# Down projection of a ViT layer: the residual add moves from VectorE into accumulating DMAs

## The reference

```
h = patches(x) @ W.T + b                        # 32 x 256 tokens x 256
h = h + attention(layernorm(h))                 # 16 heads, causal
xq = fake_quant(layernorm(h), clip_x)           # one scale for the whole tensor: max|.| over all tokens
a  = silu(xq @ q(w_gate).T) * (xq @ q(w_up).T)  # 704 hidden features
h = h + fake_quant(a, clip_down) @ q(w_down).T  # again one scale for the whole tensor
```

## Time and profile before

| | |
|---|---|
| median of 3 runs | 898.87 us (895.33 to 903.66) |
| span of the profiled execution | 901.6 us |
| pass C in that execution | about 824 to 901.6 us, 77.6 us |
| VectorE busy in pass C | 67.6 of 77.6 us |
| TensorE / ScalarE busy in pass C | 48.6 / 43.7 us |
| GpSimd busy in pass C | 0 |
| moved by DMA in pass C | 16.79 MB, mean 215 GB/s |

### The profile page before, as it was taken

How to read it: one execution, slowest core, us unless ns; L and a number is a source line. 1 busy time by engine, 2 the same in 40 slices (tenths; PEclk the granted TensorE clock), 3 DMA queues, 4 the chain that set the end, 5 groups by cost and what they waited for, 6 DMA issues and landing times. The chain is left out here.

```text
span 901.6 us, 21285 instructions
## 1 busy us (share of the span) xinstructions
PE 709.8 (79%) x6962; PEld 381.5 (42%) x6962; DVE 793.9 (88%) x1320; ACT 509.0 (56%) x748; POOL 537.5 (60%) x545
## 2 busy tenths in 40 slices
PE   3668788878888888888888888888786559996775
PEld 2444344444444444444444444444433223332453
DVE  6867688988999999999999999999996349998898
ACT  3324455555665565556655655565554438886664
POOL 1435666666777776677777766777753238882000
PEclk9686999999999999999999999999989769998999
DMA  7233445564554555555545555554544222223488
GB/s 255 64 70 84 99 106 117 119 126 103 132 119 108 120 118 120 122 128 134 119 108 120 118 121 122 126 135 90 92 89 86 50 44 50 47 47 105 137 261 254
DMA packets 245639, 102.86 MB, mean 114 GB/s; under 512 B 214496, under 2 KB 240864, under 8 KB 245600
## 3 DMA queue, kind: packets, MB, share of 16 engines
q1 hardware_dynamic: 245600, 102.37, 48.9%
HBM read 33.13 MB, written 16.78 MB: 55 GB/s over the span
## 5 line engine op out<-in xcount | busy, mean ns | idle before, releaser
L1199 DVE TENSOR_REDUCE act_all<-pair 128x8 f32<-128x1024 f32 x192 | 233.9, 1218 | 32.2 <-PE pair L551 23.2
L969 POOL TENSOR_SCALAR_AFFINE_SELECT act_all<-act_all 128x512 f32<-128x512 f32 x128 | 105.7, 836 | 104.0 <-ACT act_all L832 104.0
L832 ACT ACTIVATE act_all<-pair 128x768 f32<-128x768 f32 x128 | 104.0, 813 | 79.4 <-PE pair L568 79.4
L969 POOL TENSOR_SCALAR_AFFINE_SELECT ffn<-ffn 128x512 f32<-128x512 f32 x128 | 86.5, 676 | 97.6 <-ACT ffn L832 97.6
L832 ACT ACTIVATE ffn<-pair 128x768 f32<-128x768 f32 x128 | 102.6, 802 | 69.7 <-PE pair L568 69.6
L512 PE MATMUL pair<-act_all 128*128 128x256 f16 (+1 forms) x960 | 120.7, 281 | 5.0 <-POOL act_all L1007 3.3
L566 PE MATMUL pair<-act_all 64*128 64x256 f16 x512 | 74.3, 286 | 59.2 <-DMA act_all<-act_all 32.3
L544 PE MATMUL pair<-act_all 32*128 32x128 f16 x1536 | 78.3, 222 | 43.3 <-DMA act_all<-act_all 35.3
L512 PEld LDWEIGHTS pair<-act_all 128*128 128x128 f16 (+1 forms) x960 | 92.1, 100 | 31.2 <-issue 17.8
L1007 POOL TENSOR_TENSOR act_all<-act_all 128x1280 f16<-128x1280 f32 x31 | 82.5, 2660 | 17.9 <-ACT act_all L797 17.9
L544 PEld LDWEIGHTS pair<-act_all 32*128 32x128 f16 x1536 | 44.5, 94 | 89.9 <-issue 40.8
(11 more groups left out here) (130 smaller groups left out, 1500.8 us busy)
## 6 DMA issues: line engine op xcount, KB each, us to landing
act_all<-x_t SPq DMA_DIRECT2D x32, 640.0 KB, 4.2
out<-act_all SPq DMA_DIRECT2D x32, 256.0 KB, 2.6
ffn<-out SPq DMA_DIRECT2D x16, 512.0 KB, 4.7
out<-ffn SPq DMA_DIRECT2D x16, 512.0 KB, 3.2
act_all<-act_all SPq DMA_TRANSPOSE x192, 2.8
act_all<-w_down SPq DMA_DIRECT2D x1, 704.0 KB, 8.9
act_all<-w_emb SPq DMA_DIRECT2D x1, 640.0 KB, 3.8
ffn<-w_gate SPq DMA_DIRECT2D x1, 640.0 KB, 7.1
```

Of the source, the lines that this page charges most:

```text
L832: act.activation(probs[i // 4][:, o:o + 2, 0:3, :].rearrange("p h k s -> p h (k s)"), pair[1][:, :].rearrange("p (h c) -> p h c", h=2)[:, ...
L969: pool.affine_select(out=p, in_=p, pattern=[[0, 4], [1, P]], compare_op=ALU.is_ge, fill=0.0, base=0, channel_multiplier=-1).then_inc(maske ...
L1199: dve.tensor_reduce(to.rearrange("p (g k) -> p k g", g=GROUPS)[:, first:first + 2, :], pair[2][:, :].rearrange("p (k g t) -> p k g t", k=2 ...
```

## The change

The residual is no longer loaded into SBUF. SyncE's loads and stores of pass C are gone, and so is VectorE's add. `scale_down` writes to one of four buffers, and GpSimd issues one DMA for each group that adds this buffer to the output tensor in HBM. VectorE now quantises the first half of g+2 before it scales g, and before it writes a buffer for the second time it waits for the DMA that read it (`y_added`).

```diff
@@ -229,8 +229,7 @@
                 for k in range(2)]
         silu = [ffn[:, 2560 + 512 * k:3072 + 512 * k] for k in range(3)]
         up_sb = [ffn[:, 4096 + 512 * k:4608 + 512 * k] for k in range(2)]
-        h_in = [ffn[:, 1024 * k:1024 * (k + 1)].rearrange("p (t e) -> p t e", t=GTT) for k in range(4)]
-        scaled = ffn[:, 4096:5120]
+        scaled = [ffn[:, 1024 * k:1024 * (k + 1)].rearrange("p (t e) -> p t e", t=GTT) for k in range(4)]
 
 
         q8 = [w.rearrange("p c i -> p (c i)").bitcast(INT8) for w in (wg_t, wu_t)]
@@ -314,14 +313,12 @@
         silu_ready = sem("silu_ready")
         act_ready = sem("act_ready")
         act_peak = sem("act_peak")
-        g_loaded = [sem(f"g_loaded{k}") for k in range(4)]
         a_quantised = sem("a_quantised")
         aq_ready = sem("aq_ready")
         down_done = sem("down_done")
         down_scaled = sem("down_scaled")
-        y_ready = sem("y_ready")
         down_scale_ready = sem("down_scale_ready")
-        y_stored = [sem(f"y_stored{k}") for k in range(4)]
+        y_added = [sem(f"y_added{k}") for k in range(4)]
 
         CONSTS, FFN_WEIGHTS = 16 * 6, 16 * 7
         out_rows = out.rearrange("b (t p) e -> p b t e", p=P)
@@ -450,33 +447,8 @@
             for k in range(2):
                 sp.wait_ge(xq_turned[k], 8 * NG)
 
-            sp.wait_ge(act_ready, len(DVE_M) * NG)
-            sp.wait_ge(act_by_pool, len(POOL_M) * NG)
-
-            def load_g(g, slot):
-                sp.dma_start(h_in[slot], out_grp[:, g]).then_inc(g_loaded[slot], 16)
-
-            def store_g(turn, slot, load=True):
-
-                g = 4 * turn + slot
-                sp.wait_ge(y_ready, g + 1)
-                sp.dma_start(out_grp[:, g], h_in[slot]).then_inc(y_stored[slot], 16)
-                if load:
-                    other = (slot + 2) % 4
-                    sp.wait_ge(y_stored[other], 16 * (turn if slot < 2 else turn + 1))
-                    load_g(g + 2, other)
-
-            for g in range(4):
-                load_g(g, g)
-            for g in range(4):
-                store_g(0, g, load=(g >= 2))
-            with sp.Fori(1, NG // 4 - 1) as i:
-                for slot in range(4):
-                    store_g(i, slot)
             for slot in range(4):
-                store_g(NG // 4 - 1, slot, load=(slot < 2))
-            for slot in range(4):
-                sp.wait_ge(y_stored[slot], 16 * (NG // 4))
+                sp.wait_ge(y_added[slot], 16 * (NG // 4))
 
 
         @block.tensor
@@ -1078,6 +1050,16 @@
                 if g + 2 < NG:
                     widen_x(g + 2)
                 multiply(g, POOL_M[1])
+
+            def add_to_out(g):
+
+                pool.wait_ge(down_scaled, g + 1)
+                pool.dma_start(out_grp[:, g], scaled[g % 4], accum_op=ALU.add).then_inc(y_added[g % 4], 16)
+
+            for g in range(NG):
+                add_to_out(g)
+            for slot in range(4):
+                pool.wait_ge(y_added[slot], 16 * (NG // 4))
 
 
         @block.vector
@@ -1436,29 +1418,20 @@
                 dve.tensor_scalar(q8[k][:, lo:hi], act_all[:, bass.ds(g * A_COLS + lo, hi - lo)], small[:, 13:14],
                                   QMAX, ALU.mult, ALU.min).then_inc(a_quantised, 1)
 
-            def scale_down(g, k):
+            def scale_down(g, k, slot):
 
                 dve.wait_ge(down_done, g + 1)
-                if not isinstance(g, int) or g >= 1:
-                    dve.wait_ge(y_ready, g)
-                dve.tensor_tensor(scaled.rearrange("p (a e) -> p a e", a=GTT),
-                                  pair[k][:, :].rearrange("p (a e) -> p a e", a=GTT),
+                dve.tensor_tensor(scaled[slot], pair[k][:, :].rearrange("p (a e) -> p a e", a=GTT),
                                   down_row[:, :].rearrange("p (a e) -> p a e", a=1).to_broadcast([P, GTT, D]),
                                   ALU.mult).then_inc(down_scaled, 1)
 
-            def add_h(g, slot):
-
-                dve.wait_ge(down_scaled, g + 1)
-                y = h_in[slot].rearrange("p t e -> p (t e)")
-                dve.tensor_tensor(y, y, scaled, ALU.add).then_inc(y_ready, 1)
-
             def pass_c(turn, slot, ahead=True):
                 g, k = 4 * turn + slot, slot % 2
-                scale_down(g, k)
                 if ahead:
                     quantise(g + 2, k, 0)
-                dve.wait_ge(g_loaded[slot], turn * 16 + 16)
-                add_h(g, slot)
+                if not isinstance(turn, int) or turn >= 1:
+                    dve.wait_ge(y_added[slot], turn * 16)
+                scale_down(g, k, slot)
                 if ahead:
                     quantise(g + 2, k, 1)
 
```

## The result

The changed kernel takes 885.12 us (median of 4 runs, 884.11 to 887.06) against 900.48 us (median of 4, 895.33 to 903.66) for the kernel before in the same comparison: ratio 0.9848, 95% interval 0.9809 to 0.9887. It is 1.5% faster. I had forecast 910 us.

What follows compares the result with a forecast made beforehand. VectorE's unbroken sequence, 3.99 us a group, was taken to bound pass C; accumulating DMAs would bound it next. The end, 840.6 + 16 D with D = 4.5, gave a span of 912.6 us, 910 by the median; range 883 to 936.

Steps and rivals of the forecast that it cites:

- D: Pass C: time from one 512 KB accumulating DMA to the next; taken as 4.5 us, bounds 3.0 to 6.1 us.
- closer to three passes in turn: Pass C's accumulating DMA: read, read and write of 512 KB one after another at 1.50 us each, 4.5 us.
- the low end of my bounds: Pass C's accumulating DMA: the write overlaps the reads, two passes of 1.50 us, 3.0 us per group.
- costs nothing, both are needed once per group in either order: Pass C on VectorE: quantising the first half ahead of the scaling was priced at no cost.
- Rival 1: Pass C: the adding is hidden or nearly, so the kernel is faster, 884 to 886 us by the median; chance 0.32.
- compute-bound sum: Pass C with compute setting the pace at 2.86 us a group: span ends at 886.5 us, 15.1 under the profiled span.
- Rival 2: Pass C: VectorE and GpSimd exclude each other, so GpSimd's issue bounds; 4.37 us a group, 908 us; chance 0.24.
- 2.5 us beside the bytes: End of pass C: what one accumulating DMA takes beside its bytes, chosen between a load's 3.2 and a store's 1.7 us.
- 0.3 us to the end: End of pass C: time from the last DMA's landing to the end of the span, 0.3 us.
- Rival 3: Pass C: gain and loss cancel through partly overlapped reads and writes, D 3.25 to 4.38 us, 893 to 908 us; chance 0.12.
- Signs I had named: Pass C's profile after: VectorE idle before scaling, scalings 4.4 to 6.1 us apart, DMA share near 1, GpSimd's queue short of work.

Runs made afterwards that it cites:

- e2: The changed kernel with the accumulating DMAs and the waits on them taken out: 875.45 us, ratio 0.9700 to the kernel before.
- e4: The changed kernel with SyncE issuing plain stores of the scaled product in place of GpSimd's adds: 881.08 us, ratio 0.9800 to the kernel before.
- e5: The changed kernel with the scaling put back ahead of the first half's quantising, nothing left out: 892.66 us, ratio 0.9927 to the kernel before.
- e1: The changed kernel with its 16 adds running free from a constant SBUF region, without waits after the first scaling: 885.7 us (one run).
- e6: The kernel before with VectorE's add cut from 1024 to 2 columns, loads and stores kept: 888.38 us, ratio 0.9878 to the kernel before.
- e9: The kernel before with only the order changed, first half's quantising ahead of the scaling, full add kept: 898.69 us, ratio 1.0011 to the kernel before.
- in the second: The changed kernel compared with the kernel before once more: 886.21 us (median of 6), ratio 0.9864.
- e1b: As e1, but with plain stores in place of the accumulating DMAs: 877.48 us (one run).
- e3: The changed kernel with GpSimd issuing plain stores in place of accumulating DMAs, each waiting for its scaling: 882.70 us, ratio 0.9791 to the kernel before.
- e8: As e6, with the first half's quantising also put ahead of the scaling: 884.28 us, ratio 0.9844 to the kernel before.
- e11: e7 run again beside the changed kernel: 881.08 us (median of 5), ratio 0.9833 to the kernel before.
- e7: The changed kernel with the last two groups loaded and stored by SyncE and added by VectorE: 882.70 us, ratio 0.9799 to the kernel before.

## Why the prediction was wrong

- **What bounds the kernel: right.** VectorE's sequence set the pace, and without the add its three instructions take 2.857 us (e2, e4), for 2.85 worked out. TensorE, too, is busy 12 of 12 us in e2 (836 to 848 us), but its 24 matmuls take only 2.71 us when they run without a break (e5), and VectorE never waits for it there, so VectorE's sum is the bound by a small margin.
- **D = 4.5, "closer to three passes in turn": this step failed, and with it the sign.** I had priced the DMA as three passes of 1.50 us one after another; e1 measured 2.66 us, less than two of them, so the passes overlap, and VectorE never came to wait for a buffer. Even the low end of my bounds, 3.0 us, was too high. How an add is worked off inside the DMA engines shows in no run. I had argued that it couldn't be much below because the old load and store held a share of 0.88; but in the same measure the adds show 1.22 at 182 GB/s, so that share doesn't tell how much room there is. The rule of the Trainium skill ("Collectives: The Full Stack", Part 3) that I had set against my choice, that only the second read costs and the rate halves, came far closer: the ratio here is 1.7 to 1.8.
- **The order of quantising and scaling "costs nothing, both are needed once per group in either order": wrong.** The swap did no harm, as priced, but the order matters. With the old order the loop through ScalarE and TensorE takes 6.5 to 6.6 us for two groups (e5, e6), 3.27 to 3.28 us each. I had looked at each engine's sum and not at the loop that runs through all three. With the old order the change brings 0.71 us a group, and the swap 0.28 more (e5); over the 14 groups e5 loses 5.2 us, 1.7 of them in the last distance (3.59 against 1.92 us). The swap brings nothing while the add is there (e9).
- **Rival 1 is what happened, but its time was hit partly by luck.** It gave 884 to 886 us; 885.12 was measured. Its compute-bound sum has the pace 0.14 us too quick, 0.8 us too little from the first to the last scaling, and a last part that is 2.9 us too short (the next two points). Against these 3.7 us stands that the first scaling of the profiled execution came 6.9 us earlier than in the kernel before: 5.8 us lie ahead of pass C and 1.1 us go with the clock, neither the edit's doing. In pass C the profiles differ by 12.4 us, 11.3 without the clock's part, where Rival 1 had 15.1. The medians differ by 15.4 us in the first comparison and by 11.2 in the second.
- **Rival 2, GpSimd and VectorE in each other's way: the mechanism is there, the size was off.** I had priced it as full exclusion, 1.71 us plus the issue, with 2.66 us for the issue. Measured: the issue is 1.80 us when a quantising starts while it runs, and that quantising grows by 0.15 us (1.01 to 1.16). When none starts during it the issue is 1.28 us, also where the end of a second half still runs beside it:

```profile
869.70 0.87 DVE L1418 TENSOR_SCALAR wu_t<-act_all,small 128x1280 int8<-128x1280 f32 x1
870.08 1.28 POOL L1057 DMA_DIRECT2D out<-ffn  x1 [1.20 <-DVE ffn L1424]
```

The very first issue is an exception: it takes 2.21 us, and the quantising that starts during it stays at 1.01. The 0.15 us are 0.14 us on the pace, 2 us in all (3.00 against 2.857 in e2 and e4, and inside e1b). The Trainium skill ("SBUF — State Buffer", Who interferes with whom) speaks of a lock for the whole length of a VectorE instruction in a two-port mode; whether these instructions run in such a mode shows in no row. Here 0.15 and 0.5 us is all that either loses while quantising runs beside 1.6 of the issue's 1.80 us, so by the measurement a part of the issue at most is held up.
- **The tail.** I took 2.5 us beside the bytes and 0.3 us to the end. From the end of the last scaling, 874.66, it was 0.49 us to the issue, 6.85 us to the landing and 1.4 us more to the end of the span, 8.7 us against 5.8 forecast for D = 3.0. GpSimd's plain store in e3 lands 3.3 us after the start of its issue. The longer issue (1.30 for 0.75 us) and the slower bytes (2.66 for 1.57 us) explain 1.6 of the 3.5 us between the two; what takes the rest is open. With the last two groups done the old way the whole tail is 3.6 to 3.9 us shorter.
- **Rival 3** needed D over 3.25 us and is out with 2.66. Its lower end of 893 us is a slip: D = 3.25 gives 892.6 us of span, 890 by the median.

Signs I had named: idle time of VectorE before its scaling, released by a DMA (none), and distances of 4.4 to 6.1 us (3.00). Both speak against the forecast, as written. The third, a DMA share near 1 throughout, was there all the same (1.22), so it told nothing. For Rival 1 the distances (3.00 for about 2.9) and the idle time fit, while the last landing came 7.3 us after the end of the last scaling and not 5 to 6. For Rival 2 the stretched quantising was there, but neither a share under 0.8 nor issues back to back.

## What to carry to other kernels

Before pricing a swap of two instructions at nothing, follow the loop of buffers from the instruction through the other engines and back to it, and compare its length with the engine's busy sum: here 6.6 us for two groups against 5.7. A residual add can go into accumulating DMAs when the time that the stage takes for a group is above what they need (2.66 us for 512 KB in 1 KB rows) and enough buffers, here four, cover their landing of some 7 us; keep the last one or two pieces on a compute engine, since there that landing is on the path. Measure a DMA's own pace by letting it run free beside the unchanged compute; its busy share in the real kernel does not show the room left.

## What the runs showed beside it

- A 512 KB accumulating DMA from GpSimd: 2.66 us each when back to back (e1), 6.5 to 7.4 us from the start of the issue to the landing in the changed kernel, and the same 6.9 us for the first one, which had no earlier one beside it.
- GpSimd's issue rows: 0.75 us for a plain store, 0.80 with quantising beside it (e3); 1.28 for the accumulate, 1.80 when a quantising of VectorE starts during it, 2.21 for the very first one (changed kernel); SyncE's store takes 0.37 us (e4).
- VectorE: an instruction that needs the result of the one just ahead starts 0.18 us later than one that does not (an add 1.32 us after the scaling whose result it takes, e8 and e9, a quantising 1.14 us after a scaling in the kernel before). The two differ in operation as well, so the dependence as the cause is argued and not tested.
- The start of pass C takes 7.6 to 7.8 us in eleven of the fourteen profiles and 8.6 to 8.7 in three (the kernel before, e9, e11), so it differs between profiles of one and the same kernel (e7, e11). What differs is TensorE's granted clock: it goes from the 1.2 GHz level back to 2.4 either while the first group's 24 matmuls run, as in the changed kernel's profile, whose first matmul starts at 825.66 us, or only after them, as in the kernel before, where they run from 831.50 to 836.51 us. What decides between the two is not shown. The stretch in which the clock rose (its mean is the third column from the end, 1.00 is 2.4 GHz), first in the changed kernel, then in the kernel before:

```profile
828.07:829.07 1.00, 1.00 (x10) 0.80 (x8) 0.00 (x0) 1.00 (x2) 0.00 (x0) 0.86 0.00 0
```

```profile
837.00:838.00 1.00, 1.00 (x11) 0.84 (x9) 1.00 (x2) 0.00 (x0) 0.00 (x0) 0.90 0.00 0
```
